# A fused attention and routed feed-forward kernel: expert rows by an indirect transfer instead of a product, and two products of the router joined in one

## The reference

```python
x = x + attn(cond(x, cond_512), ...)          # 16 heads, causal, 2 null keys, layer norm, q and k normalised
x = x + ffn(cond2(x, cond_512), ...)          # cond2: a small attention over 16 groups, two scaled linear layers

# ffn, for every row xf of 256 (8192 rows):
cluster_scores = xf @ cluster_sigs.T          # 8 clusters
tile_scores = xf @ sigs.T                     # 64 experts, 8 in each cluster
cluster_idx = argmax(calibrate(cluster_scores))
local_idx = argmax(calibrate(tile_scores)[the 8 of that cluster])
tile_idx = cluster_idx * 8 + local_idx
h = gelu(xf @ compress_w1 + compress_b1)      # 256 to 64
comp = tanh(h @ compress_w2 + compress_b2)    # 64 to 2
hh = relu(comp @ spline_w1[tile_idx] + spline_b1[tile_idx])       # 16 numbers
mag = hh @ spline_w2[tile_idx] + spline_b2[tile_idx]
y = xf + mag * directions[tile_idx] * output_scale                # 256 numbers
out = layer_norm(y) * gamma + beta
```

## Time and profile before

| | |
|---|---|
| time, three runs | 1913.91, 1919.03 (median), 1920.64 us |
| the profiled execution | 1920.77 us, its span 1919.0 us |
| mean granted TensorE clock | 0.977 |
| TensorE busy | 1836.4 us, 96% of the span |
| VectorE busy | 1629.5 us, 85% |
| ScalarE busy | 1237.6 us, 64% |
| GpSimd busy | 1065.0 us, 56% |
| the chain that ended last | TensorE 93%, VectorE 4% |
| transfers | 83.09 MB, mean 43 GB/s |

### The profile page before, as it was taken

How to read it: one execution, slowest core, us unless ns; L and a number is a source line. 1 busy time by engine, 2 the same in 40 slices (tenths; PEclk the granted TensorE clock), 3 DMA queues, 4 the chain that set the end, 5 groups by cost and what they waited for, 6 DMA issues and landing times.

```text
span 1919.0 us, 63488 instructions
## 1 busy us (share of the span) xinstructions
PE 1836.4 (96%) x25286; PEld 1489.1 (78%) x25286; DVE 1629.5 (85%) x4120; ACT 1237.6 (64%) x2514; POOL 1065.0 (56%) x775
## 2 busy tenths in 40 slices
PE   4899999999999999999999999999999999999974
PEld 3688888878888887887888888788888878878762
DVE  5577888888888899888889888888988988898765
ACT  2566676666667666666766666666666676666642
POOL 0455565565565566556556655655655565565522
PEclk7899999999999999999999999999999999999985
DMA  4011122122112112112211211221121121122121
GB/s 145 9 26 37 41 46 46 40 42 44 39 44 44 37 42 44 44 38 46 42 38 44 44 44 38 41 45 40 44 44 39 40 44 44 38 47 43 44 48 28
DMA packets 337972, 83.09 MB, mean 43 GB/s; under 512 B 277007, under 2 KB 336879, under 8 KB 337903
## 3 DMA queue, kind: packets, MB, share of 16 engines
q1 hardware_dynamic: 337902, 82.12, 19.6%
HBM read 48.51 MB, written 33.55 MB: 43 GB/s over the span
## 4 chain that ended last, share of the span: by engine, by line
PE 93%; DVE 4%; POOL 1%; ACT 1%; issue 1%; SPq 0%; DMA 0%; POOLq 0%; ACTq 0%; DVEq 0%
PE pa L439 29%; PE ps L518 6%; PE pa L446 6%; PE pb L418 6%; PE ps L505 6%; PE ps L469 5%; PE ps L476 4%; PE pc L652 3%; PE pc L538 3%; PE pa L418 3%; PE ps L562 3%; PE pb L425 3%; PE pb L610 3%; PE pb L513 2%; PE ps L520 2%; PE pb L430 2%
## 5 line engine op out<-in xcount | busy, mean ns | idle before, releaser
L1106 POOL TENSOR_TENSOR yve<-ymv,eps 128x1 f32<-128x1 f32 x64 | 12.1, 190 | 547.3 <-DVE ymv L1007 547.3
L439 PE MATMUL pa<-wq,xnTs 128*128 128x512 f32 x768 | 213.4, 414 | 0.0
L439 PE MATMUL pa<-wv,y 128*128 128x512 f32 x768 | 210.4, 410 | 1.9 <-ACT kn L782 0.3
L439 PE MATMUL pa<-wk,y 128*128 128x512 f32 x768 | 211.8, 411 | 0.0
L1098 POOL TENSOR_TENSOR rn<-nrg,mhalf 128x16 f32<-128x16 f32 x64 | 203.4, 3177 | 4.2 <-DVE nrg L1055 3.7
L1086 POOL TENSOR_TENSOR rn<-nrg,mhalf 128x16 f32<-128x16 f32 x64 | 186.6, 2915 | 17.7 <-DVE nrg L1033 11.6
L439 PEld LDWEIGHTS pa<-wv,y 128*128 128x128 f32 x768 | 134.8, 188 | 32.3 <-issue 5.4
L1091 POOL TENSOR_TENSOR bd<-vm,pick 128x1024 f32<-128x1024 f32 x64 | 121.9, 1905 | 65.3 <-PE pc L652 61.5
L439 PEld LDWEIGHTS pa<-wq,xnTs 128*128 128x128 f32 x768 | 137.4, 192 | 24.9 <-ACT kcat L736 0.3
L439 PEld LDWEIGHTS pa<-wk,y 128*128 128x128 f32 x768 | 134.7, 188 | 27.8
L1103 POOL TENSOR_TENSOR pr<-pr,rden 128x1056 f32<-128x1056 f32 x64 | 135.9, 2123 | 2.9 <-DVE rden L927 2.9
(11 more groups left out here) (222 smaller groups left out, 5206.1 us busy)
## 6 DMA issues: line engine op xcount, KB each, us to landing
xT<-in_xT SPq DMA_DIRECT2D x64, 128.0 KB, 2.4
x<-in_x SPq DMA_DIRECT2D x64, 128.0 KB, 2.1
x1d<-x SPq DMA_DIRECT2D x64, 128.0 KB, 1.7
kxdr<-kxn SPq DMA_DIRECT2D x64, 128.0 KB, 1.7
vm<-kxdr SPq DMA_DIRECT2D x128, 64.0 KB, 2.8
odr<-o SPq DMA_DIRECT2D x256, 32.0 KB, 2.0
on<-odr SPq DMA_DIRECT2D x64, 128.0 KB, 2.1
xb<-x1d SPq DMA_DIRECT2D x64, 128.0 KB, 2.1
```

Source lines behind the costliest of these rows:

```text
L439: last = mm(bank, part(lhs(a_, k)), part(rhs(b_, k)), start=(n == 0), stop=(n == 3 * CK - 1))
```

## The change

The product with the one-hot matrix goes: VectorE computes the number of the expert's row (`slot`, then `row` as an unsigned integer), and GpSimd issues an indirect transfer that reads the 128 rows of 321 numbers from the table in memory straight into `gs`, which has two buffers now. `oh`, `ohT`, the table on the chip, one transpose, one product and two copies of ScalarE go. Scores and first layer are one product with the 136 columns of `wsc`; the hidden numbers are copied to `hidn`, and each second step one transpose turns those of two tiles into `hT` (128 rows, the gelu takes the bias with it), and one product with a block matrix `w2b` (128x4) gives `comp`, whose bias `b2` now goes into the tanh.

With it the stages are spread anew: `pipeline` runs to T + 9, most pieces belong to a tile one further back, and the pieces stand in another order in the `step` of every engine, as well as in SyncE's. The core of the diff:

```diff
-            for i in range(last, T + 9):
+            for i in range(last, T + 10):
...
-                    from_T(two(pb, 0), zT)
-                    for k in range(CK):
-                        mm(pb[:, C:C + NS], zT[:, k, :], wsc[:, k, 0:NS],
-                           start=(k == 0), stop=(k == CK - 1), skip_group_check=True)
-                    for k in range(CK):
-                        last = mm(pb[0:CH, C + P:C + 2 * P], wsc[:, k, NS:NS + CH], zT[:, k, :],
-                                  start=(k == 0), stop=(k == CK - 1), skip_group_check=True)
+                    from_T(two(pb, 0), zT)
+                    for k in range(CK):
+                        last = mm(pb[:, C:C + NS + CH], zT[:, k, :], wsc[:, k, :],
+                                  start=(k == 0), stop=(k == CK - 1), skip_group_check=True)
...
-                    nc.tensor.transpose(pb[:, C:C + P], oh[:, :], ident[:, :]).then_inc(S("ohT_mm"), 1)
-                    mm(pb[:, 0:GATH], ohT[:, :], gath[:, :], start=True, stop=True).then_inc(S("gathered"), 1)
+                    if p == 1:
+                        nc.tensor.transpose(pb[:, C:C + P], hidn[:, :, :].rearrange("p u h -> p (u h)"), ident[:, :])\
+                            .then_inc(S("hT_mm"), 2)
...
+                    if p == 1:
+                        mm(pb[:, C + P:C + P + 4], hT[:, :], w2b[:, :], start=True, stop=True).then_inc(S("comp_mm"), 2)
...
-                    fn(ohT[:, :], pb[0:NT, C:C + P], ACT.Copy).then_inc(S("ohT_done"), 1)
-                    fn(gs[:, :], pb[:, 0:GATH], ACT.Copy).then_inc(S("gs_done"), 1)
...
-                    v.tensor_tensor(oh[:, 0:NT].rearrange("p (c k) -> p c k", k=TPC), bc(chosen[:, p, 0, :], 2, TPC),
-                                    bc(chosen[:, 1 - p, 1, :], 1, NC), ALU.mult).then_inc(S("oh_done"), 1)
+                    v.scalar_tensor_tensor(out=slot[:, 1 - p:1 - p + 1], in0=third[:, 1 - p, 0:1], scalar=float(TPC),
+                                           in1=third[:, p, 1:2], op0=ALU.mult, op1=ALU.add).then_inc(S("slot_done"), 1)
+                    wait(dve, "slot_done", t9)
+                    v.tensor_scalar(row[:, 1 - p, :], slot[:, 1 - p:1 - p + 1], float(NT + TPC), None, ALU.add).then_inc(S("row_done"), 1)
...
+                if live(i, 9):
+                    wait(pool, "row_done", t9)
+                    g.tensor_tensor(pause[:, :], eps[:, :], eps[:, :], ALU.add)
+                    g.indirect_dma_start(out=gs[:, 1 - p, :], out_offset=None, in_=A["gath"],
+                                         in_offset=bass.IndirectOffsetOnAxis(ap=row[:, 1 - p, :], axis=0))\
+                        .then_inc(D("gathered", 1 - p), 16)
```

More of the change, by code:

```diff
@@ L276, in adaln_attention_ffn @@
         gb = sb("gb", [P, 2, C])
-        gath = sb("gath", [NT, GATH])
-        w2b = sb("w2b", [CH + 1, 2])
-        b1 = sb("b1", [CH, 1])
+        slot = sb("slot", [P, 2])
+        pause = sb("pause", [P, 1])
+        row = sb("row", [P, 2, 1], mybir.dt.uint32)
+        third = sb("third", [P, 2, 2])
+        w2b = sb("w2b", [2 * CH, 4])
+        b1 = sb("b1", [2 * CH, 1])
+        b2 = sb("b2", [P, 2])
         CO = {}
@@ L489, in step @@
[L489 to L499, removed]
@@ L516, in step @@
[L516 to L526, removed]
@@ L556, in step @@
[L556 to L564, removed]
@@ new lines, in step @@
+                if live(i, 4):
+                    wait(pe, "oT_done", t4)
+                if live(i, 5):
+                    wait(pe, "kxT_done", t5)
+                    from_T(two(pb, 0), kxT).then_inc(S("kxn_mm"), 1)
+                if live(i, 3):
+                    for r, t, s in HEADS:
+                        last = sim_tile(r, t, s)
+                    last.then_inc(S("sim_shared"), 1)
+                    wait(pe, "sim_shared", t3)
+                if live(i, 6):
+                    wait(pe, "a_done", t6)
@@ L655, in step @@
                     last.then_inc(S("av_mm"), 1)
+                if live(i, 3):
+                    wait(pe, "pr_add", t3)
+                if live(i, 4):
+                    for r in range(4):
+                        mm(ps[:, 2, C:2 * C], oT[:, r, :], wout[:, r, :], start=(r == 0), stop=False)
+                if p == 1:
+                    if live(i, 8):
+                        wait(pe, "gelu_done", t8)
+                if live(i, 7):
+                    linear_T(two(pb, C), wo2, om).then_inc(S("zT_mm"), 1)
@@ new lines, in step @@
+                if live(i, 2):
+                    wait(pe, "qT0_done", t2)
+                    wait(pe, "kn_done", t2)
+                    four(pa[:, 0, :], kn, 0)
+                if live(i, 6):
+                    wait(pe, "o2_done", t6)
+                if live(i, 5):
+                    wait_dma(pe, "v2_in", t5, 1 - p, 2)
+                    for h in range(2):
+                        last = nc.tensor.transpose(pc[:, h * P:(h + 1) * P], vm[:, 1 - p, h * P:(h + 1) * P], ident[:, :])
+                    last.then_inc(S("mix_kT"), 1)
@@ new lines, in step @@
+                if live(i, 2):
+                    four(pa[:, 1, :], kn, 4).then_inc(S("kT1_mm"), 1)
+                if live(i, 4):
+                    for r in range(4, HP):
+                        mm(ps[:, 2, C:2 * C], oT[:, r, :], wout[:, r, :], start=False, stop=False)
+                    for s in range(BT):
+                        last = mm(ps[s * L:(s + 1) * L, 2, C:2 * C], pnT[:, s * L:(s + 1) * L], nullw[:, s, :],
+                                  start=False, stop=True)
+                    last.then_inc(S("out_mm"), 1)
```

731 lines of the change are left out of this document (363 added, 368 removed).

## The result

The changed kernel takes 2048.8 us (median of four, 2046.2 to 2052.8) against 1918.4 (1913.9 to 1920.6): ratio 1.0685, 95% interval 1.0657 to 1.0712. It is slower, as forecast, but by 130 us where the forecast had 51, and outside its range (1865 to 2005).

What follows compares the result with a forecast made beforehand. VectorE was to become the bound at 24.2 + 4.75 = 28.95 us a tile against 28.15 before; over 54 intervals that is 43 us, plus 8 for fill and drain, 51 in all: 1970 us forecast, range 1865 to 2005.

Steps and rivals of the forecast that it cites:

- The bound and the lock: VectorE becomes the bound; large GpSimd operations and certain VectorE operations from SBUF exclude each other, costing 4.75 us a tile.
- The `over` term: After `k_guard`, VectorE's next `over`, with two SBUF inputs, waits for GpSimd's product on `kn`: 1.7 us a tile.
- For `yT` I had 1.0 + 1.75: Behind `rden`: first `y` waits 1.0 us for GpSimd's scaling of `pr`, second 1.75 for its spread into `bd`.
- scalings by a column pass freely: VectorE's scalings by a column, like reductions and PSUM operations, are not blocked by large GpSimd operations.
- if the `y` writes last 0.3 us beside the scaling: Sign of being wrong: VectorE's `y` writes unblocked beside GpSimd's scaling of `pr`; expected were 1.2 to 2.0 us.
- TensorE alone would need 26.7 us: TensorE's time a tile after the removed transposes, copies' products and matmuls save it 1.46 us.
- TensorE waits 2.2 us a tile: With VectorE as the bound at 28.95 us, TensorE waits at `pn` and `yT`, 2.2 us a tile.
- Fill and drain, I take 8: The pipeline gets one step more, costing 5 to 14 us in all, taken as 8.
- Its landing is hidden: The indirect transfer's rows are read about 9 us after `row`, so its landing costs nothing.
- The issue of the indirect transfer: GpSimd's issue falls in its free 2.2 us before `rden`, under 2.4 us long; cost taken as 0.
- The delay that the prediction quotes: GpSimd cannot write descriptors while VectorE holds the shared ports: issue 2.5 us longer, sum up to 54 us higher, 2024.
- The other side: Rival: losses around `yT` and `over` don't arise, TensorE stays the bound at 26.7 us a tile, 1848 us; chance 0.14.

Runs made afterwards that it cites:

- e9: Changed kernel with q's second half projected twice on TensorE and 8 of the 32 small products on `pr` left out: 1997.8 us (1.0422).
- e2: Changed kernel with GpSimd's spread into `bd` moved behind its product on `kn`, and VectorE's `yn` behind the sums with `alibi`: 1920.0 us (1.0011).
- e5: Changed kernel with VectorE's `over` and `yn` ahead of `qn`, and GpSimd's spread between its power operations for q and `yn`: 1871.0 us (0.9746).
- e7: Changed kernel with multiplication and column sum of `yT` in one step from PSUM, the clamps in the operations behind: 1996.4 us, measured once.
- e8: Kernel before the change, with the product that fetches the expert rows cut from 321 columns to 16: 1893.6 us (0.9870).
- e4: Changed kernel with the indirect transfer left out, each tile taking constant expert rows: 2016.3 us (1.0507).
- e3: Changed kernel with VectorE's three operations on `over` and its `yn` moved ahead of `qn`: 1974.8 us (1.0296).
- e10: Changed kernel with six of TensorE's smallest products (64x64) done again in each tile: 2069.0 us (1.0789).
- e1: Changed kernel with TensorE projecting q's second half twice, ahead of the wait for `yT`: 2167.2 us (1.1297).
- e6: Changed kernel with three long matmuls (128x512) added ahead of q's last projection: 2181.6 us (1.1365).

## Why the prediction was right and wrong

The 129.7 us of span divide so: 91.0 in the 47 steady tiles (30.06 against 28.12 us), 11.5 up to the 11th `rden`, 27.2 behind the 58th.

- **The bound and the lock: right.** "VectorE needs 24.2 + 4.75 = 28.95 us a tile": 28.90 in the tiles at full clock, 28.94 in e9. That is 0.82 x 47 = 38.5 us; the forecast had 43 for 54 intervals. e2 and e5 show the cause: the same work in another order takes 27.58 and 26.83.
- **Its terms.** The `over` term, 1.7, measured 1.6 in the tile shown (1.87 against 0.29), `nrg` 0.3 as put. For `yT` I had 1.0 + 1.75; the pair costs 3.1 (3.58 against 0.48). The reason was wrong: "scalings by a column pass freely" fell to the rows of after and to e7. No row of before showed one from SBUF beside a large GpSimd operation; they ran there by chance, which is no evidence. Its sign of being wrong, "if the `y` writes last 0.3 us beside the scaling", came up in half: `y` takes 0.29, but behind the scaling and the spread. That the loss came out near its size, one operation earlier, is in part luck.
- **"TensorE alone would need 26.7 us": right,** with 26.5 and 27.2 in turn in e5. How much of it each removed piece gave is not shown; e8 gave less for the narrower product (0.46) than such estimates by width have (0.68).
- **"TensorE waits 2.2 us a tile": right, and taken for harmless. This is the step that failed.** The sum put TensorE's durations at the full clock in a kernel where it no longer works without a break. The wait at `yT` lowers the granted clock in 35 of 47 tiles; the matmuls behind it take up to twice as long until it is back, and since VectorE then waits for them (1.08 us at `xm` and 0.51 at `sc`), the loss is on the path. Such a tile takes 30.46 us where all of e9 take 28.94: 35 x 1.52 = 53 us, and e9 gives back 51. The prediction put this at nothing. Every row of before from the steady part had a clock of 1.00.
- **"Fill and drain, I take 8": 38.7. This is the second term that failed.** 12.8 of it are the indirect transfer (e4). "Its landing is hidden" holds for steady tiles, but in the last three VectorE waits 2.5, 3.5 and 3.4 us for the rows, since nothing is left to lie beside. e5, which waits for the rows just as long, is 0.5 above the kernel before up to the 11th `rden` and 13.9 behind the 58th. The 24 us between it and the changed kernel went with the two moves, so they are again lock and clock, in the thinner steps that I had counted as free of them; how they divide is not shown.
- **The issue of the indirect transfer: short, but not free.** It takes 1.06 us or less in 55 of the 64 and 1.27 to 1.44 in nine near the two ends, and costs the tile itself 0.14 us. Yet e4 gives back 32.5 us in all, where the sum had 0. The delay that the prediction quotes from the Trainium skill, "SBUF — State Buffer", section "SBUF: two separate sides", by which the sum would have been up to 54 us higher, does not show. It was hardly put to the test: beside the issue VectorE does one product of about 0.5 us (`zT`) and the sum `den`.
- **The rivals.** The other side, TensorE as the bound at 26.7 and 1848 us, lay 23 us from e5. It needed one operation of GpSimd and VectorE's `over` and `yn` elsewhere.

## What to carry to other kernels

List the large GpSimd operations and what VectorE does beside each; put PSUM reads and reductions there, and leave room between rivals for the lock: with 0.04 to 0.07 us between their starts the order flipped from tile to tile (e3), with 0.7 it did not (e5). When a change makes TensorE wait, price not only the wait but its matmuls behind it at half clock; if the wait can't go, work that nobody needs may fill it at a gain, but of the three fillers here one gained 51 us and two lost 118 and 133. Price a latency "hidden" in the steady state once more for the last tiles.

## What was unexpected of the hardware

- The clock fell behind waits of 1.5 to 1.95 us in 35 of 47 tiles, behind 1.1 and 1.4 us in 18 of 47 (e7), behind 1.15 and 1.6 in 34 (e10), behind 0.9 and 1.1 in none (e3). The same wait did it in one tile and not in the next, and a longer wait did not always do it more often. What decides is open.
- Two of the programs (e1, e6) moved 9 more packets of 16 KB on the instruction queue in each round of the loop, with stands of TensorE of 3.8 and 1.7 us in the round of e1 that is shown; a program with more matmuls (e10) did not, nor did e9. Why is open.
- An indirect transfer of 128 rows of 1284 bytes: 1.06 us on GpSimd, and 3.6 us (median) from issue to landing, more than the 2.0 us fixed that the prediction names.
